# Attention row maxima carried from partitions into a row by DMA instead of TensorE transposes and a ScalarE copy

## The reference, cut to what matters

```python
qkv = hidden_states @ qkv_w.T + qkv_b
...
xq = xq * scale[None, None, None, :]
scores = jnp.einsum('bqhd,bkhd->bhqk', xq, xk)
probs = jax.nn.softmax(scores.astype(jnp.float32), axis=-1).astype(xq.dtype)
out = jnp.einsum('bhqk,bkhd->bqhd', probs, xv)
```

## Time and profile before

| | |
|---|---|
| device time, median of 3 runs | 2070.34 us (2069.89, 2070.34, 2188.6) |
| the profiled execution's own time | 2067.07 us |
| its span, from first to last instruction | 2065.3 us |
| mean granted clock of TensorE | 0.943 of full speed |
| TensorE matmul, weight load | 1855.6 us (90%), 912.9 us (44%) |
| VectorE, ScalarE, GpSimd | 1378.7 us (67%), 1135.1 us (55%), 979.1 us (47%) |
| DMA packets | 22875, 32.01 MB, 5.3% of the 16 engines' span on queue 1 |

### The profile page before, as it was taken

How to read it: one execution, slowest core, us unless ns; L and a number is a source line. 1 busy time by engine, 2 the same in 40 slices (tenths; PEclk the granted TensorE clock), 3 DMA queues, 4 the chain that set the end, 5 groups by cost and what they waited for, 6 DMA issues and landing times.

```text
span 2065.3 us, 27531 instructions
## 1 busy us (share of the span) xinstructions
PE 1855.6 (90%) x9556; PEld 912.9 (44%) x9556; DVE 1378.7 (67%) x2925; ACT 1135.1 (55%) x1507; POOL 979.1 (47%) x763
## 2 busy tenths in 40 slices
PE   3799999988999799998999988998899989998863
PEld 2444453443644344453554435444364434444342
DVE  4466756667576776756578585766657676677656
ACT  1367755655466554655456554665546654575422
POOL 2065545634554444652645345563465535463621
PEclk7799999999999999998999999999899999999895
DMA  4020000000200000010200000010010000000000
GB/s 150 1 62 1 1 1 1 12 21 1 62 11 1 1 21 1 1 32 0 62 11 1 1 0 21 1 32 0 11 41 1 1 0 21 1 1 1 21 0 10
DMA packets 22875, 32.01 MB, mean 15 GB/s; under 512 B 2577, under 2 KB 16977, under 8 KB 22737
## 3 DMA queue, kind: packets, MB, share of 16 engines
q1 hardware_dynamic: 22736, 30.26, 5.3%
HBM read 13.48 MB, written 4.19 MB: 9 GB/s over the span
## 4 chain that ended last, share of the span: by engine, by line
PE 70%; DVE 18%; issue 5%; ACT 4%; POOL 2%; DMA 0%; SPq 0%; POOLq 0%; DVEq 0%; ACTq 0%
PE attended L955 19%; PE key_scores L935 18%; PE misc L853 7%; PE misc L995 5%; PE max_scores L903 5%; DVE relu L1432 3%; PE misc L1019 3%; PE misc L965 2%; PE misc L921 2%; PE misc L1051 1%; PE misc L1010 1%; PE misc L1040 1%; PE misc L858 1%; DVE prob_sum L1446 1%; DVE buf_b L1328 1%
## 5 line engine op out<-in xcount | busy, mean ns | idle before, releaser
L1189 ACT ACTIVATE probs<-key_scores 128x1024 f32<-128x1024 f32 x512 | 524.5, 1024 | 602.1 <-PE key_scores L935 420.6
L1792 POOL TENSOR_TENSOR prob_sum<-prob_sum,probs 128x512 f32<-128x512 f32 x384 | 538.9, 1403 | 234.0 <-ACT probs L1189 212.8
L955 PE MATMUL attended<-probs,v_all 128*64 128x512 f32 x2048 | 577.1, 637 | 0.1
L1432 DVE CUSTOM_DVE_ANT_0 relu<-max_scores,relu 128x512 f32<-128x512 f32 x512 | 332.3, 686 | 263.7 <-PE max_scores L903 262.6
L935 PE MATMUL key_scores<-q_high,k_chain 64*128 64x512 f32 x2048 | 470.2, 455 | 10.7 <-ACT probs L1189 10.3
L935 PEld LDWEIGHTS key_scores<-q_high,k_chain 64*128 64x128 f32 x2048 | 197.4, 189 | 468.3 <-issue 251.5
L1446 DVE TENSOR_TENSOR prob_sum<-prob_sum,probs 128x512 f32<-128x512 f32 x384 | 375.6, 978 | 19.6 <-ACT probs L1189 8.9
L1173 ACT ACTIVATE relu<-max_scores 128x1024 f32<-128x1024 f32 x256 | 261.5, 1021 | 47.2 <-PE max_scores L903 47.2
L903 PE MATMUL max_scores<-k_max,q_high 64*128 64x512 f32 x1024 | 215.5, 416 | 75.4 <-DVE row_max L1432 73.9
L1788 POOL TENSOR_TENSOR prob_sum<-probs 128x512 f32<-128x512 f32 x64 | 87.8, 1371 | 345.6 <-PE misc L965 286.6
L935 PE MATMUL key_scores<-q_low,k_chain 64*128 64x512 f32 x1024 | 207.8, 402 | 0.0
(11 more groups left out here) (406 smaller groups left out, 2170.5 us busy)
## 6 DMA issues: line engine op xcount, KB each, us to landing
k_chain<-k_chain SPq DMA_DIRECT2D x32, 256.0 KB, 3.8
buf_a<-in_x SPq DMA_DIRECT2D x8, 512.0 KB, 4.9
k_max<-k_max SPq DMA_DIRECT2D x16, 256.0 KB, 3.7
x_in<-in_x SPq DMA_DIRECT2D x7, 512.0 KB, 4.2
out_x<-buf_b SPq DMA_DIRECT2D x7, 512.0 KB, 3.0
heads_out<-in_qkv_wT SPq DMA_DIRECT2D x1, 1536.0 KB, 8.5
wo<-in_o_wT SPq DMA_DIRECT2D x1, 1024.0 KB, 12.7
rows_sb<-in_rows SPq DMA_DIRECT2D x1, 646.0 KB, 10.4
```

The costliest lines, as they stand in the source:

```text
L955: tensor.matmul(attended[head * HD:(head + 1) * HD, :], v_all[:, kt, g * HD:(g + 1) * HD], prob_slot(u, kt, head), start=kt == 0, stop=kt ...
L1189: scalar.activation(probs[(u * KT + kt) % len(probs)][:, :, :], key_scores[:, :, :], ACT.Exp).then_inc(S["exp"])
L1432: vector.tensor_tensor_reduce(out=relu[:, head, :], in0=max_scores[:, head, :], in1=relu[:, head, :], scale=1.0, scalar=-3.4e38, op0=ALU.a ...
L1792: gpsimd.tensor_tensor(prob_sum[1][:, :], prob_sum[1][:, :], probabilities, ALU.add).then_inc(S["prob_sum1"])
```

## The change

The maxima go from `row_max` to `shift_row` by two DMAs of 2 KB on SyncE's queue, one for each head. `row_max` is now laid out so that the four maxima of a partition lie side by side, and a DMA writes partition after partition: `shift_row` has the maxima in the order (partition, block), four apart for neighbouring queries. The shift matmul reads them with a step of four elements. The sign moves into `shift_ones` (-1). `shift_row` has two buffers; the stage starts 4 steps ahead; `max_T` and ScalarE's copy are gone, and so is their place in the ring of three banks. `crowded` is set by `shift` in step 4 of 8, where it was step 6.

```diff
@@ -71,7 +71,7 @@
                "directions": (SMALL, D)}
 
 
-Q_AHEAD, MAX_AHEAD, SHIFT_AHEAD, PV_BEHIND, FINISH_BEHIND = 14, 11, 2, 2, 4
+Q_AHEAD, MAX_AHEAD, SHIFT_AHEAD, PV_BEHIND, FINISH_BEHIND = 14, 11, 4, 2, 4
 HALF_AHEAD = 5
 FIRST_HALF, SECOND_HALF = CHUNKS - 1, CHUNKS
 JOBS = CHUNKS + 1
@@ -94,7 +94,7 @@
 
 NT_TIMES = "tiles"
 SIGNALS = {
-    "ones": {"ones": 1}, "minus_half": {"minus_half": 1}, "padding": {"padding": 7},
+    "ones": {"ones": 1}, "minus_half": {"minus_half": 1}, "padding": {"padding": 6},
     "x_stats": {"bn_stats": NT, "moments": NT, "var_eps": 1, "rstd": 1}, "x_norm": {"normed": NT},
     "x_T": {"x_T": 1}, "x_split": {"xT_high": 1, "xT_low": 1},
     "split_q": {"weights_high": 1, "weights_low": 1}, "split_k": {"weights_high": 1, "weights_low": 1},
@@ -104,7 +104,7 @@
     "v_proj": {"v_proj": 1}, "v_split": {"v_all": 1},
     "q_proj": {"q_proj": 1}, "q_split": {"q_high": 1, "q_low": 1},
     "max_d": {"max_d": 2, "relu": 1}, "max_s": {"max_s": 2, "row_max": 2},
-    "max_T": {"max_T": 1}, "max_rows": {"max_row": 1},
+    "max_rows": {"max_row": 32},
     "scores": {"key_scores": 2, "exp": 1}, "attend": {"attended": 2}, "raw_out": {"raw_out": 1},
     "add": {"prob_sum0": 1, "prob_sum1": 1},
     "sums": {"sums": 1}, "inv": {"ln_sum": 1, "inv_sum": 1}, "heads": {"heads_out": 1},
@@ -130,7 +130,7 @@
 
 BANK_FREE = {
     "x_T": ("xT_low", "x_split", 0), "k_proj": ("k_full", "k_split", 0), "v_proj": ("v_all", "v_split", 0),
-    "q_proj": ("q_low", "q_split", 0), "max_T": ("max_row", "max_rows", 0), "sums": ("ln_sum", "inv", 0),
+    "q_proj": ("q_low", "q_split", 0), "sums": ("ln_sum", "inv", 0),
     "k2": ("k2T", "k2T", 0), "v2": ("v2_block", "v2_block", 0), "out_proj": ("x1", "x1", 0),
     "norm_T": ("normT", "norm_ev", 0), "q2": ("q2_done", "q2_ev", 0), "scores2": ("soft2", "soft2", 2),
     "attended2": ("out2T", "out2", 0), "weights2T": ("p2T", "p2T", 0), "projected2": ("x2", "x2", 0),
@@ -235,9 +235,8 @@
 
 
 def shift(plan, u):
-    plan.put_in_bank("max_T", u)
-    yield LATE
     plan.put("max_rows", u)
+    yield
 
 
 def finish(plan, u):
@@ -665,9 +664,9 @@
         v_all = sb("v_all", [P, KT, KV * HD])
         q_high = [sb(f"q_high{i}", [P, CH], F32R) for i in range(3)]
         q_low = [sb(f"q_low{i}", [P, CH], F32R) for i in range(3)]
-        shift_row = sb("shift_row", [P, CH], F32R)
+        shift_row = [sb(f"shift_row{i}", [P, CH], F32R) for i in range(2)]
         shift_ones = sb("shift_ones", [P, P], F32R)
-        row_max = [sb(f"row_max{i}", [P, NT, HD + 1]) for i in range(2)]
+        row_max = [sb(f"row_max{i}", [P, 2, NT]) for i in range(2)]
         relu = sb("relu", [P, 2, 512])
         probs = [sb(f"probs{i}", [P, 2, CH]) for i in range(3)]
         prob_sum = [sb(f"prob_sum{i}", [P, CH]) for i in range(2)]
@@ -835,7 +834,16 @@
                     sync.dma_start(k_chain[to:to + HD, 1, :, half, cols].bitcast(F32),
                                    k_chain[at:at + HD, 0, :, half, cols].bitcast(F32)).then_inc(S["k_swap"], 16)
 
-            stages = {"load": load, "load_x": load_x, "k_swap": k_swap, "residual": residual, "store": store}
+            def max_rows(u):
+                sp.wait_ge(*after("row_max", "max_s", u, NT - 1))
+                sp.wait_ge(*after("key_scores", "scores", u - 2, 0))
+                sp.wait_ge(*after("padding", "padding"))
+                for head in range(2):
+                    row = shift_row[u % 2][head * HD:head * HD + 1, :].bitcast(F32)
+                    sync.dma_start(row,
+                                   row_max[u % 2][:, head, :]).then_inc(S["max_row"], 16)
+
+            stages = {"load": load, "load_x": load_x, "k_swap": k_swap, "max_rows": max_rows, "residual": residual, "store": store}
             for stage, *key in plan.entries:
                 if stage in stages:
                     stages[stage](*key)
@@ -910,16 +918,6 @@
             def max_s(u, i):
                 pe.wait_ge(*freed("max_s", u, i))
                 max_pair(u, i, 512, "max_s")
-
-            def max_T(u):
-                ps = bank("max_T", u)
-                pe.wait_ge(*after("row_max", "max_s", u, NT - 1))
-                pe.wait_ge(*after("padding", "padding"))
-                pe.wait_ge(*freed("max_T", u))
-                pe.wait_ge(*loaded("consts"))
-                for i in range(NT):
-                    done = tensor.transpose(ps[0:HD + 1, i * P:(i + 1) * P], row_max[u % 2][:, i, :], ident)
-                done.then_inc(S["max_T"])
 
             def scores(u, kt):
                 _, _, b, g = unit(u)
@@ -941,7 +939,7 @@
                     pe.wait_ge(*after("padding", "padding"))
                     for head in range(2):
                         rows = slice(head * HD, (head + 1) * HD)
-                        tensor.matmul(key_scores[:, head, :], shift_ones[rows, :], shift_row[rows, :],
+                        tensor.matmul(key_scores[:, head, :], shift_ones[rows, :], shift_row[u % 2][rows, :].rearrange("k (p i) -> k i p", i=NT),
                                       start=False, stop=True, skip_group_check=True).then_inc(S["key_scores"])
 
             def attend(u, kt):
@@ -1101,7 +1099,7 @@
 
             stages = {
                 "x_T": x_T, "k_proj": k_proj, "v_proj": v_proj, "q_proj": q_proj, "max_d": max_d,
-                "max_s": max_s, "max_T": max_T,
+                "max_s": max_s,
                 "scores": scores, "attend": attend, "sums": sums, "k2": k2, "v2": v2, "out_proj": out_proj,
                 "norm_T": norm_T, "q2": q2, "scores2": scores2, "attended2": attended2, "weights2T": weights2T,
                 "projected2": projected2, "route": route, "compress": compress, "comp": comp, "pickT": pickT,
@@ -1172,13 +1170,6 @@
                     act.wait_ge(*after("row_max", "max_s", u - 1, NT - 1))
                 scalar.activation(relu[:, :, :], max_scores[:, :, :], ACT.Relu).then_inc(S["relu"])
 
-            def max_rows(u):
-                act.wait_ge(*after("max_T", "max_T", u))
-                act.wait_ge(*after("key_scores", "scores", u - 1, 0))
-                act.wait_ge(*after("padding", "padding"))
-                scalar.activation(shift_row[0:HD + 1, :], bank("max_T", u)[0:HD + 1, :], ACT.Copy,
-                                  scale=-1.0).then_inc(S["max_row"])
-
             def scores(u, kt):
                 last_u, last_kt = prob_before(u, kt)
                 act.wait_ge(*after("key_scores", "scores", u, kt))
@@ -1295,7 +1286,7 @@
 
             stages = {
                 "x_split": x_split, "scale_q": scale_q, "k_split": k_split, "k_high": k_high, "q_split": q_split,
-                "max_d": max_d, "max_rows": max_rows, "scores": scores, "raw_out": raw_out_, "inv": inv, "k2T": k2T_, "norm_ev": norm_ev, "q2_ev": q2_ev,
+                "max_d": max_d, "scores": scores, "raw_out": raw_out_, "inv": inv, "k2T": k2T_, "norm_ev": norm_ev, "q2_ev": q2_ev,
                 "exp2": exp2, "p2T": p2T, "out2": out2, "route_ev": route_ev, "gelu": gelu, "tanh_exp": tanh_exp,
                 "cal_exp": cal_exp, "pickT_ev": pickT_ev, "gathered_ev": gathered_ev,
             }
@@ -1425,14 +1416,13 @@
             def max_s(u, i):
                 done = before("max_s", "max_s", u, i)
                 dve.wait_ge(*after("relu", "max_d", u, i))
-                dve.wait_ge(*after("max_T", "max_T", u - 2))
-                dve.wait_ge(*after("padding", "padding"))
+                dve.wait_ge(*after("max_row", "max_rows", u - 2))
                 for head in range(2):
                     dve.wait_ge(S["max_s"], done + head + 1)
                     vector.tensor_tensor_reduce(
                         out=relu[:, head, :], in0=max_scores[:, head, :], in1=relu[:, head, :], scale=1.0, scalar=-3.4e38,
                         op0=ALU.add, op1=ALU.max,
-                        accum_out=row_max[u % 2][:, i, HD * head:HD * head + 1]).then_inc(S["row_max"])
+                        accum_out=row_max[u % 2][:, head, i:i + 1]).then_inc(S["row_max"])
 
             def add(u, kt):
                 probabilities = prob_slot(u, kt, 0)
@@ -1735,14 +1725,14 @@
                 gpsimd.memset(minus_half[:, :], -0.5).then_inc(S["minus_half"])
 
             def padding():
-                zeroed = [row_max[0][:, :, :], row_max[1][:, :, :], shift_row[:, :].bitcast(F32),
+                zeroed = [shift_row[0][:, :].bitcast(F32), shift_row[1][:, :].bitcast(F32),
                           shift_ones[:, :].bitcast(F32), v2_block[:, :, :, :, :]]
                 for n, view in enumerate(zeroed):
                     pool.wait_ge(S["padding"], n)
                     gpsimd.memset(view, 0.0).then_inc(S["padding"])
                 for n, row in enumerate((0, HD)):
                     pool.wait_ge(S["padding"], len(zeroed) + n)
-                    gpsimd.memset(shift_ones[row:row + 1, :].bitcast(F32), 1.0).then_inc(S["padding"])
```

(1 more changed line is left out.)

## The result

The changed kernel takes 2124.23 us (median of 4, 2122.77 to 2125.8), against 2070.11 for the kernel before on the same chip: ratio 1.0273, 95% interval 1.0258 to 1.0287. (One of the four executions before, 2188.6 us, fell into a slower state of the chip and is left out of the ratio.) Forecast were 2050 us and a range of 2030 to 2088. The profiled execution has a span of 2121.8 us, against 2065.3.

The account below looks back on a forecast made before the run. TensorE was taken as the bound, with the loop of scores and exponential on top. From 2067 us, minus 31 (transposes) plus 12 (stepped read) gave 2048, forecast as a median of 2050 us, range 2030 to 2088.

Parts of the forecast that it names:

- Moved: the tail's pieces: Tail beside the attention units: later pieces come a step earlier or later; 0, with 15 us either way.
- The last sentence of the prediction: If time changes, the shift pair stays and no DMA wait shows, it is the tail's place, seen in row-maxima waits.
- The transposes: TensorE, ahead of each unit's shift: removing the four transposes gains 31 us, between 15 and 37.
- The stepped read: Shift matmul on TensorE reading every fourth column: 12 us of loss, between 0 and 49.
- rival 2: Shift matmul: stepped reads cost as much as the slowest pair, 44 us instead of 12, median 2083 us; chance 10%.
- rival 1: Shift matmul: stepped reads cost nothing, median 2039 us; chance 17%.
- The DMAs: Two added DMAs on SyncE and the wait for them: landing in 3.2 us is hidden, 0; upper end 14 us.
- rival 3: DMAs of the maxima land late, units wait between scores and shift; at 10 us landing, median 2136 us; chance 12%.
- The ring: The bank going back to the ring of three gives its other users more room: 0.
- ScalarE's copy: Removed copy on ScalarE, 37.7 us busy but not on the path: gain 0 us, bounds 0 and 5.
- Rival 4: The tail falls badly: TensorE waits 15 to 25 us more for maxima, 2065 to 2075 us; chance 13%.

Follow-up runs that it names:

- before_moved_tail: The kernel before, transposes kept, with only the rule for `crowded` changed (step 4 counts, step 6 not), so tail pieces stand as in the changed kernel: 2127.48 us, 1.0286.
- start_2_steps: The changed kernel with stage `shift` starting 2 steps ahead instead of 4, so every tail piece stands in its old step: 2064.47 us, ratio 0.9985.
- all_tails_pause_1: start_2_steps with each tail pausing 1 step ahead of its second layer norm, so feed-forward halves come later: 2100.6 us, 1.0166.
- the thin pair: thin_calibration and thin_moved_tail, the same cut of VectorE's calibration with tails in the old and the moved place: 1979.38 and 2020.65 us, 41 us apart.
- thin_moved_tail: The changed kernel (tails moved) with VectorE's calibration cut from 18 instructions to 3 in each of a tail's two calibrations: 2020.65 us, 0.9781.
- thin_calibration: start_2_steps with VectorE's calibration cut from 18 instructions to 3 in each of a tail's two calibrations, pieces in place: 1979.38 us, 0.9574.

## Why the prediction was wrong

**The step that failed is "Moved: the tail's pieces".** I put it at 0 with 15 us either way; it costs 60, by two pairs: before_moved_tail against the kernel before (59.9), and the changed kernel against start_2_steps (59.8). Two errors are in it. I followed the rule of `crowded` for the first two `ALONE` pieces and stopped. In three tails the third then runs into steps where preparations hold the lane, and comes five steps later. And I bounded the cost by a quarter of one wait, that of TensorE for row maxima, as if moved pieces could only touch that. The last sentence of the prediction named this case, but looked for it in that wait alone. The pair start_2_steps and changed kernel, which differ in the place of the tails (and of `shift`) alone, shows where it went. First the page of start_2_steps, then TensorE's longest waits in it:

```profile
PE 1839.2 (89%) x9300; PEld 883.1 (43%) x9300; DVE 1389.4 (67%) x2925; ACT 1105.6 (54%) x1443; POOL 975.0 (47%) x762
```

```profile
PE max_scores L911 <- DVE row_max L1422: 73.7, 24, 7.5
PE misc L866 <- DVE buf_b L1319: 22.3, 8, 4.1
PE key_scores L933 <- ACT probs L1180: 10.2, 18, 2.5
```

Of 62.5 us of span (2059.3 to 2121.8), 37.5 are more idle TensorE: 23.0 the wait for row maxima, 5.4 that for norms, 8.5 that for the exponential, and smaller ones. The other 25.0 are the same 9300 matmuls being busy longer. The granted clock fell from 0.944 to 0.936, since it is at half for a while at each wait of over 3 us. From the two means, with half as the lower level, it was at half for 272 us instead of 231, an estimate; that makes at most 20 of the 25 us, and the rest is not explained. I had priced neither the other waits nor the clock.

How the calibration's waits grow shows in the last tail of the loop. Its calibration has two halves. In start_2_steps TensorE waits for row maxima 2.65 us behind the first and 4.30 behind the second, and then finds the picked tiles (L1088) ready:

```profile
1895.72 0.80 PE L911 MATMUL max_scores<-k_max,q_high 64*128 64x512 f32 x2 [2.65 <-DVE row_max L1422]
...
1913.02 0.79 PE L911 MATMUL max_scores<-k_max,q_high 64*128 64x512 f32 x2 [4.30 <-DVE row_max L1422]
...
1913.74 1.06 PE L1088 MATMUL misc<-consts_sb,buf_c 128*64 128x128 f32 x4
```

In all_tails_pause_1 TensorE waits 6.14 us for row maxima behind the first half, and 4.52 us for the picked tiles themselves behind the second:

```profile
1940.65 0.80 PE L913 MATMUL max_scores<-k_max,q_high 64*128 64x512 f32 x2 [6.14 <-DVE row_max L1424]
...
1941.38 1.98 PE L955 MATMUL attended<-probs,v_all 128*64 128x512 f32 x4
...
1944.30 0.63 PE L935 MATMUL key_scores<-q_high,k_chain 64*128 64x512 f32 x2
...
1955.46 1.06 PE L1090 MATMUL misc<-consts_sb,buf_c 128*64 128x128 f32 x4 [4.52 <-DVE buf_c L1655]
1956.45 1.98 PE L955 MATMUL attended<-probs,v_all 128*64 128x512 f32 x4
```

Behind both long waits the clock is at half, its lower level (attended in 1.98 us, where it takes 1.08 at full). That is the calibration's part, 19 us by the thin pair.

For the other 41 the thin pair has the waits without the calibration. Of the 39.4 us between its spans (1978.0 and 2017.4) 30.5 are more idle TensorE: 15.9 the wait for row maxima (32.2 to 48.1), 7.0 that for the exponential, 5.5 that for GpSimd's weights of the cross-attention, 5.4 that for norms. One piece behind them can be named, the tail's second layer norm. Beside unit 21 VectorE scales four tiles for it (L1319). In start_2_steps this comes behind the row maxima, and TensorE waits 1.64 us for the norm:

```profile
667.02 0.69 DVE L1422 CUSTOM_DVE_ANT_0 relu<-max_scores,relu 128x512 f32<-128x512 f32 x1
...
668.24 5.41 DVE L1319 TENSOR_SCALAR buf_b<-buf_a,moments,rstd 128x256 f32<-128x256 f32 x4
...
673.70 1.11 PE L866 MATMUL misc<-consts_sb,buf_b 128*128 128x128 f32 x4 [1.64 <-DVE buf_b L1319]
```

In the changed kernel, one step later, it stands ahead of the row maxima:

```profile
680.78 5.49 DVE L1319 TENSOR_SCALAR buf_b<-buf_a,moments,rstd 128x256 f32<-128x256 f32 x4 [1.25 <-POOL rstd L1745]
686.19 0.68 DVE L1422 CUSTOM_DVE_ANT_0 relu<-max_scores,relu 128x512 f32<-128x512 f32 x1
...
687.54 0.80 PE L911 MATMUL max_scores<-k_max,q_high 64*128 64x512 f32 x2 [5.61 <-DVE row_max L1422]
```

Such waits stand in units 21, 37, 53 and 61, 5.6, 5.6, 3.6 and 3.6 us in the changed kernel and in thin_moved_tail alike, and thin_calibration has none there: together they are as long as the growth of the wait for row maxima in the thin pair. No run moves the norm alone, so its price is read from waits and not measured. What stays open are the other pieces, and whether a place can be told good or bad without running it.

**The transposes: 31 forecast, 17 measured** together with copy and DMAs (13 to 21). The term was mis-sized. I had counted on nothing else being late next. In the lean stretch of the changed kernel the relu of the maxima is: it ends at 195.38, the next pair of maxima starts at 195.44, 0.33 behind the scores' last pair at 195.11 instead of the 0.23 that the pair takes, and the step lasts from 194.55 to 196.87, 2.32 us and not 2.14. That is 0.18 of the 0.58 given back. If all 64 units were like this one, it would be 11.5 us, an estimate; beside tails it wasn't followed. Even in start_2_steps TensorE is busy only 16.4 us less than before, where I had forecast 25 to 45. The wait of weight loads for relu went from 10.0 us in 22 places before to 19.1 in 44 in start_2_steps. The removal let TensorE reach the maxima before ScalarE had emptied their banks.

**The stepped read: 12 forecast, 14.3 measured** (9 to 19). I had it from the row at half clock; the slowest pair, rival 2, and no cost, rival 1, are out. The Trainium skill, SBUF — State Buffer, section "Door 1: The DMA port swizzle", says that each access that goes to a new line of 16 bytes pays. These traces agree in kind, with 0.44 us for the moving pair in place of 0.24 and 306 ns for a load in place of 184.

**The DMAs: 0 forecast, no wait seen.** They land in 2.0 us, at most 4.2, within the 6.7 that I counted; rival 3, on which I had put the slow side, did not come. **The ring:** 0, as forecast within what can be told. **ScalarE's copy:** forecast 0, not measured by itself; it is part of the 17.

**Rival 4** named the right place, but its 15 to 25 us are a quarter to two fifths of the 60, because it took its price from the same wait. The terms add up as far as they can be tested: 2064 (start_2_steps, all of the change but the moved tail) and the 60 us that the moved tail costs in the kernel before give 2124, and 2124.23 were measured. That 2067 - 17 + 14 is 2064 tests nothing, since the 17 and the 14 come from the same three runs.

## What to carry to other kernels

In a kernel whose order comes from a planner, compute the two plans and compare them entry by entry before pricing an edit: a rule that looks at what else starts in a step can move work that the edit never names, and here that was worth more than all that the edit was about. A tuned order of long chains beside a loop has no slope to extrapolate: one step later cost 36 us, and 1 to 4 earlier 31. When work is taken off the busiest engine, look at the buffers that it reaches sooner, and count only what the next one leaves.

## What the runs showed of the hardware

Some of VectorE's instructions take up to four times as long when they start while GpSimd is at work on a large tile. With the tails moved, the calibration beside unit 54 met GpSimd's sums. From the changed kernel's timeline:

```profile
1716.67 0.39 DVE L1601 TENSOR_REDUCE buf_c<-buf_c 128x32 f32<-128x224 f32 x1
...
1719.45 1.60 POOL L1782 TENSOR_TENSOR prob_sum<-prob_sum,probs 128x512 f32<-128x512 f32 x1
1719.85 1.45 DVE L1611 TENSOR_TENSOR buf_c<-buf_c 128x224 f32<-128x224 f32 x1
1721.13 1.31 POOL L1791 TENSOR_TENSOR heads_out<-raw_out,inv_sum 128x512 f32<-128x512 f32 x1
1721.33 1.36 DVE L1615 TENSOR_TENSOR buf_c<-buf_c,rows_sb 128x224 f32<-128x224 f32 x1
1722.52 2.67 POOL L1782 TENSOR_TENSOR prob_sum<-prob_sum,probs 128x512 f32<-128x512 f32 x2
1722.73 0.39 DVE L1618 TENSOR_REDUCE buf_c<-buf_c 128x32 f32<-128x224 f32 x1
1723.15 0.92 DVE L1615 TENSOR_TENSOR buf_c<-buf_c,knot_step 128x224 f32<-128x224 f32 x1
```

and the same instructions in start_2_steps, beside unit 62, where GpSimd is idle until 1907.15:

```profile
1905.35 0.39 DVE L1611 TENSOR_TENSOR buf_c<-buf_c 128x224 f32<-128x224 f32 x1
1905.78 0.39 DVE L1615 TENSOR_TENSOR buf_c<-buf_c,rows_sb 128x224 f32<-128x224 f32 x1
1906.20 0.39 DVE L1618 TENSOR_REDUCE buf_c<-buf_c 128x32 f32<-128x224 f32 x1
```

L1611 and L1615 take 1.45 and 1.36 us: both begin while an instruction of GpSimd runs and end 0.25 us behind its end (1721.05 and 1722.44). With GpSimd idle they take 0.39. The reduction beside GpSimd keeps its 0.39. The instruction of the last layer norm at L1693 shows it over the whole span (busy, mean ns), in start_2_steps and in the changed kernel:

```profile
L1693 DVE SCALAR_TENSOR_TENSOR buf_b<-buf_b,moments,rows_sb 128x256 f32<-128x256 f32 x28 | 14.7, 585 | 0.0
```

```profile
L1693 DVE SCALAR_TENSOR_TENSOR buf_b<-buf_b,moments,rows_sb 128x256 f32<-128x256 f32 x28 | 23.1, 882 | 0.0
```

In the first 3 of the 28 take 1.22 us or more, in the second 12, each begun while GpSimd was at work on 128x384 or 128x512 values; the others keep 0.47 or 0.48, those beside GpSimd's instruction on 128x4 values among them. VectorE's busy time rises by 24.7 us (1389.4 to 1414.1) with the same 2925 instructions. So the place of a piece also changes its length, which is one more reason why the cost of a move can't be read off the old trace. And a DMA of 128 pieces of 16 bytes into one partition lands 2.0 us after its issue (1.8 to 4.2).
